# One-hots of every fourth column of an edge sort: from VectorE to ScalarE

## The chip, the cores and the metric

The kernel runs on one core of a Trainium2 chip. Five engines work there, each through its own queue of instructions in a fixed order, and they wait for each other by semaphores: PE (TensorE, matrix products into the PSUM banks), DVE (VectorE), ACT (ScalarE), POOL (GpSimd, here mostly gathers by indirect DMA) and SP (SyncE, which issues the other DMAs). The metric is the device time of one execution in microseconds, median of several.

## The reference, cut to what matters

Two graph layers run on 6,250 nodes with 256 features. The first is graph attention over 100,000 edges with 8 heads, the second attention over 131,072 other edges with 4 heads of 4 channels, whose result gates four experts' feed-forward networks. Both sum over the edges that end in a node:

```python
alpha = jax.nn.leaky_relu(a_src[src] + a_dst[dst], NEG_SLOPE)
ex = jnp.exp(alpha - amax[dst])
denom = jax.ops.segment_sum(ex, dst, num_segments=N)
attn = ex / (denom[dst] + 1e-16)
msg = h[src] * attn[:, :, None]
out = jax.ops.segment_sum(msg, dst, num_segments=N)
```

The first graph's edges come sorted by `dst`, the second's don't. The kernel sorts them itself, so that each chunk of 128 edges belongs to one tile of nodes. The sort doesn't depend on the first layer's result.

## The kernel before, in words

**Graph 1's loop.** The first layer runs over 104 groups of 8 chunks, one group a pass (`for i in range(NG1 + 1)` in every engine's program). POOL gathers the source rows of the 8 chunks (L722). DVE makes the scores of the pass (L1495 to L1517), ACT takes their exp (L870), and DVE multiplies the gathered rows by it in one instruction (L1523, `messages`). Then PE makes for each chunk one product that sums the messages by node (L1268), and DVE adds it to the accumulator (L1489, `add`). An add stands two chunks behind its product, so the last two adds of a pass come after the next scores. ACT also copies the transposes that PE makes of the next pass's selection matrices (L875). Of the 2,345 lines, `a` is ACT's queue, `v` DVE's and `pe` PE's.

**Graph 2's sort rides along.** `sort_order` lists the sort's steps with a cost for each, and a planner spreads them over 792 slots, one slot for each chunk of graph 1's first 99 passes (`sort_slots`). Every engine runs through the same slots, and takes from each step what is its own. In the last part of the sort there are 1,024 columns of 128 edges; a step there costs 400, and a slot gets two of them, now and then three.

**A column** j is placed by two matmuls (`place`, L1150 with 512 and L1151 with 64 columns) that multiply a one-hot of each edge's lane (`Av`) by a one-hot of its chunk's number (`Bv`), scaled by `bE`, which packs the edge's fields. `Av` comes four columns at a time: PE makes the codes into a bank ("hot", L1142), from a transpose that it makes for 16 columns ("turn", L1135, cast by ACT in L789), and ACT turns the bank into `Av` by a relu (L795). `Bv` is one instruction of DVE for each column (L2134, `onehots`): is the number 0 to 575 equal to `winF`, times `bE`.

**What sets the order.** `onehots` j stands two steps ahead of `place` j. There are four buffers `Bv`, so it waits (`p_pl`) until `place` j - 4 has read the same one. `place` j waits for its `Bv` (`v_bv`) and for its `Av` (`a_av`). Hot g stands in step 4g + 2, and needs the bank that ACT's relu of hot g - 1 has read. In each queue the sort's steps of a slot stand right behind the chunk's own work, and the exp and the copy of a pass stand ahead of its eight slots on ACT.

Of the kernel before, what the change touches and what calls it, by code (L numbers as in the profile page):

```python
# [13 lines left out]
HW = 576  # L14
# [22 lines left out]
def build(nc, x_d, src_d, dst_d, W_d, as_d, ad_d, bias_d, lns_d, lnb_d, Wg_d, gas_d, gad_d, bg_d, gam_d, bet_d,  # L37
          W1_d, b1_d, W2_d, b2_d, ei_d, out_d):
    f32, i32, u32, i16, u16, f16, b16 = (mybir.dt.float32, mybir.dt.int32, mybir.dt.uint32, mybir.dt.int16, mybir.dt.uint16,
                                          mybir.dt.float16, mybir.dt.bfloat16)  # L40
    ALU = mybir.AluOpType
    ACT = mybir.ActivationFunctionType
# [3 lines left out]
    with ctx:  # L46
        def sb(name, shape, dt=f32):
            return ctx.enter_context(nc.sbuf_tensor(name, shape, dt))
# [4 lines left out]
        def sem(name):  # L53
            return ctx.enter_context(nc.semaphore(name))

        def sems(names):
            return [sem(n) for n in names.split()]
# [39 lines left out]
        x_f = sb("x_sb", [128, T * D])  # L97
# [25 lines left out]
        ones = sb("ones", [128, 128])  # L123
# [3 lines left out]
        iota16 = sb("iota16", [128, NC2], f16)  # L127
# [71 lines left out]
        NB = 4  # L199
# [17 lines left out]
        laneI, winF, bE, u2 = x_f[:, 7808:8832].bitcast(i32), x_f[:, 8832:9856], x_f[:, 9856:10880], x_f[:, 10880:11904]  # L217
# [3 lines left out]
        nI, fI, fJ, fX, fY = xtmp(4, i32), xtmp(1, i32), xtmp(2, i32), xtmp(4, f32), xtmp(5, f32)  # L221
        Av = [x_f[:, 256 * n:256 * n + 256].bitcast(f16) for n in range(4)]
        Bv = [x_f[:, 1024 + 288 * n:1312 + 288 * n].bitcast(b16) for n in range(NB)]
        dcd = [x_f[:, 2176 + HW * n:2176 + HW * n + HW] for n in range(6)]

        def turn_at(k):

            return 5 * k + 2

        def hot_at(g):  # L230

            return 5 * (g // 4) + g % 4 + 3

        def hot_bank(g):

            return pbank[7 if g < HB // 4 + 2 else 5]
# [44 lines left out]
                e.wait_ge(v_out, outs(n))  # L281


        l_e1, l_e2, l_w, l_row, l_blk, p_tm, s_map1, s_map2, p_hot = sems("l_e1 l_e2 l_w l_row l_blk p_tm s_map1 s_map2 p_hot")
        l_h = sems("l_h0 l_h1 l_h2 l_h3")
        s_c, s_v, s_stage, s_cnt, p_tot, s_pair, s_flag, s_fold = sems(
            "s_c s_v s_stage s_cnt p_tot s_pair s_flag s_fold")
# [15 lines left out]
        s_lane, v_bv, a_av, p_pl, s_idx2 = sems("s_lane v_bv a_av p_pl s_idx2")  # L303
# [481 lines left out]
        def a_sort(a, op):  # L785
            if op[0] == "turn":
                k = op[1]
                a.wait_ge(p_hot, turn_at(k))
                a.copy(CT[k % 2], hot_bank(4 * k)[:, 0:128]).then_inc(a_av, 1)  # L789
            if op[0] == "hot":  # L790
                g = op[1]
                a.wait_ge(p_hot, hot_at(g))
                if g >= 4:
                    a.wait_ge(p_pl, 4 * (g - 3))
                a.activation(Av[g % 4], hot_bank(g)[:, :], ACT.Relu).then_inc(a_av, 1)  # L795

        def a_ffn(a, op):
            if op[0] == "up" and op[3] == 1:
# [300 lines left out]
        def p_sort(pe, op):  # L1099
            if op[0] == "cmask":  # L1100
                b = op[1]
                pe.wait_ge(v_mk, b + 1)
                for h in range(2):
                    t = pe.matmul(pbank[5 + h][:, :], Z16[:, 48 - b:176 - b], msk[b % 3][:, HB * h:HB * h + HB], start=b == 0, stop=b == T - 1)
                t.then_inc(p_mk, 1)
            if op == ("offsets", 0):
                pe.wait_ge(s_dg, 1)
                pe.matmul(pbank[7][:, 0:2 * T], ones[:, :], dg.rearrange("p w b -> p (w b)"), start=True, stop=True).then_inc(p_tot2, 1)
            if op[0] == "map":
                p_map_row(pe, g2, s_tm2, 1, (5, 6, 7))  # L1110
            if op[0] == "pmask":
                b = op[1]
                pe.wait_ge(v_mk, T + b + 1)
                if b == 0:
                    pe.wait_ge(s_base, 1)
                    pe.wait_ge(s_map2, 6)
                for h in range(2):
                    n = 2 * b + h
                    if n >= 3:
                        pe.wait_ge(v_pk, n - 2)  # L1120
                    pe.matmul(pbank[5 + n % 3][:, :], tri16, msk[(T + b) % 3][:, HB * h:HB * h + HB], start=True, stop=False)
                    pe.matmul(pbank[5 + n % 3][:, :], selq[:, b:b + 1].broadcast_to([128, 128]), base16[:, HB * h:HB * h + HB],
                              start=False, stop=True).then_inc(p_ps, 1)
            if op == ("codes", 8):
                pe.wait_ge(s_lane, 1)
                pe.matmul(pbank[7][:, 0:128], laneT.rearrange("p j b -> p (j b)"), ident16[:, :], start=True, stop=True).then_inc(p_hot, 1)
            if op[0] == "turn":
                k = op[1]
                if k == 0:
                    pe.wait_ge(s_lane, 2)  # L1130
                else:
                    pe.wait_ge(a_av, turn_at(k) - 2)
                if k == HB // 16 + 1:
                    pe.wait_ge(s_lane, 3)
                pe.matmul(hot_bank(4 * k)[:, 0:128], C16[k // 32][:, k % 32 * 128:k % 32 * 128 + 128], ident16[:, :],  # L1135
                          start=True, stop=True).then_inc(p_hot, 1)
            if op[0] == "hot":
                g = op[1]
                pe.wait_ge(a_av, hot_at(g) - 2)
                if g == HB // 4 + 2:  # L1140
                    pe.wait_ge(s_lane, 3)
                pe.matmul(hot_bank(g)[:, :], CT[g // 4 % 2], lanes[:, g % 4 * 512:g % 4 * 512 + 512], start=True, stop=True).then_inc(  # L1142
                    p_hot, 1)
            if op[0] == "place":
                j = op[1]
                n, w = j % NB, j // HB
                A = Av[j // 4 % 4][:, j % 4 * 128:j % 4 * 128 + 128]
                pe.wait_ge(v_bv, j + 1)
                pe.wait_ge(a_av, hot_at(j // 4 + (1 if j == HB else 0)) - 1)
                pe.matmul(pbank[5 + 2 * w][:, :], A, Bv[n][:, 0:512], start=j % HB == 0, stop=j % HB == HB - 1)  # L1150
                pe.matmul(pbank[6][:, 64 * w:64 * w + 64], A, Bv[n][:, 512:HW], start=j % HB == 0,  # L1151
                          stop=j % HB == HB - 1).then_inc(p_pl, 1)
# [797 lines left out]
        def v_sort(v, c, op, tile_counts):  # L1950
# [174 lines left out]
            if op == ("fields", 6):  # L2125
# [1 line left out]
                v.memset(g2.dl[:, :], 512.0).then_inc(*c.one())  # L2127
                v.memset(g2.dl16[:, :], 512.0).then_inc(*c.one())
                v.wait_ge(*c.now())
            if op[0] == "onehots":  # L2130
                j = op[1]
                if j >= NB:
                    v.wait_ge(p_pl, j - NB + 1)
                v.tensor_scalar(Bv[j % NB], iota16[:, 0:HW], winF[:, j:j + 1], bE[:, j:j + 1], ALU.is_equal, ALU.mult).then_inc(v_bv, 1)  # L2134
# [211 lines left out]
```

## Time and profile before

| | |
|---|---|
| time, median of 3 runs | 3172.53 us (3170.5 to 3176.74) |
| the profiled execution | 3174.1 us, span 3172.3 us |
| busy, share of the span | PE 74%, DVE 70%, POOL 59%, ACT 29% |
| graph 1's multiplies (L1523) | 104, from 159.9 to 1761.0 us |
| one-hots of chunk numbers (L2134) | 1,024 from 639.6 to 1662.3 us, 404.2 us in all |
| matmuls that use them (L1150) | 1,024, 396.9 us in all |

The trace gives for each instruction its start, its duration and what ended the idle time before it. "x2" is two instructions in one row, whose time is from the start of the first to the end of the last. Groups give the number of instructions, their busy time and the mean of one, and the idle time of the engine just before them. "Windows" are the busy times of each engine in a stretch, with the clock granted to PE, 1.00 being its full 2.4 GHz.

### The profile page before, as it was taken

The page shows a single profiled execution, that of the slowest core. Times are in us where ns is not written, and L with a number is a line of the kernel's source. Part 1 is how long each engine was busy: PE and PEld are TensorE (multiplying, and loading weights), DVE is VectorE, ACT ScalarE, POOL GpSimd, SP SyncE. Part 2 cuts the span into 40 slices and gives each one's busy share as a digit, 9 for nine tenths or more (in the row PEclk, how much of TensorE's full clock was granted, in tenths as well). Part 3 has the DMA queues.
Part 4 walks back from the last instruction along what each step waited for, and adds up shares of the span by engine and source line. Part 5 has one row for each costly group of instructions (what it writes and reads, how often), then busy time and mean ns, then how long its engine had stood idle before and what let it go on. Part 6 is the DMA issues. An engine that isn't in the chain of part 4 may idle for free. (4 is left out here: it accounts for less than half of the span.)

```text
span 3172.3 us, 41404 instructions
## 1 busy us (share of the span) xinstructions
PE 2356.1 (74%) x11166; PEld 1458.1 (46%) x11166; DVE 2228.5 (70%) x5853; ACT 904.8 (29%) x2255; POOL 1882.1 (59%) x1969
## 2 busy tenths in 40 slices
PE   2777776588888878888886675987788777887745
PEld 1444444344444444444444354544455444454434
DVE  7688887877777777777776775365566555656558
ACT  6510000022222212222220453333334332333313
POOL 0557666555555555555556225677777777777740
PEclk9888875688888878888886776998899988989877
DMA  4423333233333333333335101222323322222257
GB/s 148 131 82 104 92 99 85 72 86 86 86 84 86 86 84 86 84 86 86 83 84 154 34 4 23 78 66 59 75 60 73 73 58 60 64 62 67 63 166 273
DMA packets 168323, 271.99 MB, mean 86 GB/s; under 512 B 45430, under 2 KB 87988, under 8 KB 168084
## 3 DMA queue, kind: packets, MB, share of 16 engines
q0 software_dynamic: 67008, 127.12, 17.6%
q1 hardware_dynamic: 101076, 142.09, 13.8%
q8 instruction: 100, 1.64, 0.2%
q14 instruction: 139, 1.14, 0.1%
HBM read 228.24 MB, written 40.84 MB: 85 GB/s over the span
## 5 line engine op out<-in xcount | busy, mean ns | idle before, releaser
L722 POOL DMA_INDIRECT Gb<-table,idx x832 | 977.0, 1174 | 664.6 <-PE pb L1268 424.2
L1268 PE MATMUL pb<-Gb,Sall 128*128 128x264 f32 x1664 | 679.3, 521 | 238.4 <-DVE Gb L1523 182.5
L1268 PEld LDWEIGHTS pb<-Gb,Sall 128*128 128x128 f32 x1664 | 366.0, 248 | 378.5 <-DVE Gb L1523 203.2
L1489 DVE TENSOR_TENSOR big<-big,pb 128x264 f32 x832 | 352.6, 424 | 222.3 <-PE pb L1268 115.8
L1165 PE MATMUL pb<-big,early 128*128 128x512 f32 (+1 forms) x832 | 446.5, 643 | 50.8 <-ACT Gb L805 39.8
L1179 PE MATMUL pb<-early,Gb 128*128 128x256 f32 x1568 | 442.1, 430 | 48.0 <-ACT Gb L805 46.3
L2134 DVE TENSOR_SCALAR x_sb<-iota,x_sb 128x576 bf16<-128x576 f16 x1024 | 404.2, 428 | 93.8 <-PE pb L1151 89.2
L1150 PE MATMUL pb<-x_sb 128*128 128x512 bf16 x1024 | 396.9, 438 | 0.3 <-DVE x_sb L2134 0.3
L1179 PEld LDWEIGHTS pb<-early,Gb 128*128 128x128 f32 x1568 | 318.5, 214 | 128.4 <-ACT Gb L805 49.9
L656 POOL DMA_INDIRECT dl<-table,idx x288 | 282.5, 981 | 105.9 <-issue 93.9
L656 POOL DMA_INDIRECT tab<-table,idx x272 | 267.7, 984 | 85.2 <-issue 81.7
L656 POOL DMA_INDIRECT early<-table,idx x272 | 267.0, 982 | 82.9 <-issue 82.9
L795 ACT ACTIVATE x_sb<-pb 128x512 f16<-128x512 f32 x256 | 152.9, 597 | 538.1 <-PE pb L1142 535.4
L2201 DVE TENSOR_TENSOR idx<-pb,b2B 128x256 f32<-128x256 f32 x196 | 83.2, 424 | 301.5 <-PE pb L1179 301.1
L1523 DVE TENSOR_TENSOR Gb<-Gb 128x2048 f32<-128x2048 f32 x104 | 237.5, 2284 | 0.3 <-ACT Gb L870 0.3
L2273 DVE TENSOR_TENSOR acc<-acc,asall 128x20 f32 x832 | 149.9, 180 | 117.5 <-issue 21.3
L1252 PE MATMUL pb<-early,STb 128*128 x832 | 119.3, 197 | 145.9 <-DVE zc L1511 55.7
L805 ACT ACTIVATE Gb<-pb,b1c 128x512 f32<-128x512 f32 (+1 forms) x208 | 137.0, 662 | 315.1 <-PE pb L1165 314.4
L1151 PE MATMUL pb<-x_sb 128*128 128x64 bf16 x1024 | 212.7, 208 | 0.0
L870 ACT ACTIVATE Gb<-zb 128x64 f32<-128x64 f32 x104 | 26.7, 256 | 555.8 <-DVE zb L1517 555.8
L1165 PEld LDWEIGHTS pb<-big,early 128*128 128x128 f32 x832 | 134.5, 202 | 104.3 <-ACT Gb L805 48.2
L1252 PEld LDWEIGHTS pb<-early,STb 128*128 128x128 bf16 x832 | 80.1, 97 | 213.8 <-issue 185.5
(412 smaller groups left out, 3368.6 us busy)
## 6 DMA issues: line engine op xcount, KB each, us to landing
Sall<-dlT SPq DMA_DIRECT2D x208, 256.0 KB, 3.5
Y<-idx SPq DMA_DIRECT2D x96, 256.0 KB, 2.1
big<-Y SPq DMA_DIRECT2D x16, 1024.0 KB, 10.9
Gb<-table,idx POOLq DMA_INDIRECT x832
x_sb<-in_x_dram SPq DMA_DIRECT2D x8, 1536.0 KB, 13.7
out_dram<-x_sb SPq DMA_DIRECT2D x24, 256.0 KB
dl<-table,idx POOLq DMA_INDIRECT x288
tab<-table,idx POOLq DMA_INDIRECT x272
```

The lines of the kernel that those rows point to most:

```text
L656: g.indirect_dma_start(out=Gt2[s][:, k, :], out_offset=None, in_=g2.table, in_offset=bass.IndirectOffsetOnAxis(ap=g2.idx[:, c:c + 1], axis ...
L722: g.indirect_dma_start(out=G1[:, i % 2, k, :], out_offset=None, in_=g1.table, in_offset=bass.IndirectOffsetOnAxis(ap=g1.idx[:, c:c + 1], a ...
L795: a.activation(Av[g % 4], hot_bank(g)[:, :], ACT.Relu).then_inc(a_av, 1)
L1150: pe.matmul(pbank[5 + 2 * w][:, :], A, Bv[n][:, 0:512], start=j % HB == 0, stop=j % HB == HB - 1)
L1151: pe.matmul(pbank[6][:, 64 * w:64 * w + 64], A, Bv[n][:, 512:HW], start=j % HB == 0, stop=j % HB == HB - 1).then_inc(p_pl, 1)
L1165: t = pe.matmul(pbank[b][:, 0:nt * 128], W1s[:, w, k, f * 128:f * 128 + 128], xT[:, t0:t0 + nt, k * 128:k * 128 + 128], start=k == 0, stop ...
L1179: t = pe.matmul(pbank[b][:, 0:D], hh[:, bi % 2, f, j * 128:j * 128 + 128], W2s[:, w, f, :], start=f == 0, stop=f == 3)
L1252: t = pe.matmul(pbank[1][:, k * 48:k * 48 + 48], ST1[:, i % 2, k, :], tab31s[:, bass.ds(pe.snap(regs[k], min_val=0, max_val=T * 16), 16), ...
L1268: pe.matmul(sbank[c % 3][:, 0:g1.R], S1[:, (i - 1) % 2, k, :], G1[:, (i - 1) % 2, k, :], start=True, stop=True).then_inc(p_sum, 1)
L1489: v.tensor_tensor(o, o, sbank[n % 3][:, 0:g1.R], ALU.add).then_inc(v_add, 1)
L1523: v.tensor_tensor(hv, hv, G1[:, s, :, 256:264].unsqueeze(3).broadcast_to([128, CG, 8, 32]), ALU.mult).then_inc(v_msg, 1)
L2134: v.tensor_scalar(Bv[j % NB], iota16[:, 0:HW], winF[:, j:j + 1], bE[:, j:j + 1], ALU.is_equal, ALU.mult).then_inc(v_bv, 1)
```

## The change

For every column j with j % 4 = 3 ACT makes the one-hot, by three operations on 576 elements a partition: |winF - n|, then relu(1 - that), which is 1 where the numbers agree and 0 elsewhere, then times `bE`. Two temporaries, `winA` and `winB`, are shared by all columns. Each operation waits for the one before by a new semaphore `a_bv`, and the third for the same buffer as before, `Bv[3]`. DVE leaves these columns out, and PE waits for `a_bv` there.

```diff
+        winA, winB = x_f[:, 10880:11456], x_f[:, 11456:11744].bitcast(f16)
...
                 a.activation(Av[g % 4], hot_bank(g)[:, :], ACT.Relu).then_inc(a_av, 1)
+            if op[0] == "onehots" and op[1] % 4 == 3:
+
+                j = op[1]
+                if j == 3:
+                    a.wait_ge(s_lane, 2)
+                a.activation(winA, iota16[:, 0:HW], ACT.Abs, scale=-1.0, bias=winF[:, j:j + 1]).then_inc(a_bv, 1)
+                a.wait_ge(a_bv, 3 * (j // 4) + 1)
+                a.activation(winB, winA, ACT.Relu, scale=-1.0, bias=ones[:, 0:1]).then_inc(a_bv, 1)
+                a.wait_ge(a_bv, 3 * (j // 4) + 2)
+                if j >= NB:
+                    a.wait_ge(p_pl, j - NB + 1)
+                a.activation(Bv[3], winB, ACT.Copy, scale=bE[:, j:j + 1]).then_inc(a_bv, 1)
...
-                pe.wait_ge(v_bv, j + 1)
+                if j % 4 == 3:
+                    pe.wait_ge(a_bv, 3 * (j // 4) + 3)
+                else:
+                    pe.wait_ge(v_bv, 3 * (j // 4) + j % 4 + 1)
...
-            if op[0] == "onehots":
+            if op[0] == "onehots" and op[1] % 4 < 3:
```

**ACT's queue**, the whole of the pass whose multiply starts at 924.80 us in the trace (exp, copy, hot, turn, three hots, and the exp of the next), before:

```order
L870 ACTIVATE Gb<-zb 128x8x8 [waits v_z]
L875 CAST Sall<-pb 128x1024 [waits p_sum,p_tp]
L795 ACTIVATE x_sb<-pb 128x512 [waits p_pl,p_hot]
L789 CAST x_sb<-pb 128x128 [waits p_hot]
L795 ACTIVATE x_sb<-pb 128x512 [waits p_pl,p_hot] x3
L870 ACTIVATE Gb<-zb 128x8x8 [waits v_z]
```

The same pass after the change, up to its third hot (a hot is L796 now, the turn's cast L790, the exp L883):

```order
L883 ACTIVATE Gb<-zb 128x8x8 [waits v_z]
L888 CAST Sall<-pb 128x1024 [waits p_sum,p_tp]
L796 ACTIVATE x_sb<-pb 128x512 [waits p_pl,p_hot]
L790 CAST x_sb<-pb 128x128 [waits p_hot]
L802 ACTIVATE x_sb<-iota,x_sb 128x576
L804 ACTIVATE x_sb<-x_sb,ones 128x576 [waits a_bv]
L808 ACTIVATE x_sb<-x_sb 128x576 [waits p_pl,a_bv]
L796 ACTIVATE x_sb<-pb 128x512 [waits p_pl,p_hot]
L802 ACTIVATE x_sb<-iota,x_sb 128x576
L804 ACTIVATE x_sb<-x_sb,ones 128x576 [waits a_bv]
L808 ACTIVATE x_sb<-x_sb 128x576 [waits p_pl,a_bv]
L796 ACTIVATE x_sb<-pb 128x512 [waits p_pl,p_hot]
```

Between the turn and the next exp stand four triples and three hots in turn; the fourth triple is the last thing ahead of the exp. Other passes have three or four triples, and the places of turn and hots shift from pass to pass.

**DVE's queue**, from the multiply of that pass on, before (L1482 loads registers, L1488 and L1489 are an add):

```order
L1523 TENSOR_TENSOR Gb<-Gb 128x8x256 [waits a_ex]
L2134 TENSOR_SCALAR x_sb<-iota,x_sb 128x576 [waits p_pl] x4
L1482 TENSOR_LOAD tmr
L1488 ISA [waits v_add,p_sum]
L1489 TENSOR_TENSOR big<-big,pb 128x264
L2134 TENSOR_SCALAR x_sb<-iota,x_sb 128x576 [waits p_pl] x2
L1488 ISA [waits v_add,p_sum]
L1489 TENSOR_TENSOR big<-big,pb 128x264
L2134 TENSOR_SCALAR x_sb<-iota,x_sb 128x576 [waits p_pl] x2
```

And after:

```order
L1539 TENSOR_TENSOR Gb<-Gb 128x8x256 [waits a_ex]
L2150 TENSOR_SCALAR x_sb<-iota,x_sb 128x576 [waits p_pl] x3
L1498 TENSOR_LOAD tmr
L1504 ISA [waits v_add,p_sum]
L1505 TENSOR_TENSOR big<-big,pb 128x264
L2150 TENSOR_SCALAR x_sb<-iota,x_sb 128x576 [waits p_pl] x2
L1504 ISA [waits v_add,p_sum]
L1505 TENSOR_TENSOR big<-big,pb 128x264
L2150 TENSOR_SCALAR x_sb<-iota,x_sb 128x576 [waits p_pl]
```

Every other slot has one one-hot in place of two; nothing else on DVE moved.

**PE's queue**, the first slot of that pass, before:

```order
L1268 MATMUL pb<-Gb,Sall 128x264 [waits v_add,a_w32,v_msg]
L1150 MATMUL pb<-x_sb 128x512 [waits a_av,v_bv]
L1151 MATMUL pb<-x_sb 128x64
L1142 MATMUL pb<-x_sb 128x512 [waits a_av]
L1150 MATMUL pb<-x_sb 128x512 [waits a_av,v_bv]
```

And after:

```order
L1284 MATMUL pb<-Gb,Sall 128x264 [waits v_add,a_w32,v_msg]
L1166 MATMUL pb<-x_sb 128x512 [waits a_av,v_bv]
L1167 MATMUL pb<-x_sb 128x64
L1155 MATMUL pb<-x_sb 128x512 [waits a_av]
L1166 MATMUL pb<-x_sb 128x512 [waits a_av,a_bv]
```

PE's order is the same; every fourth placing matmul waits for ACT in place of DVE, and it is the next one behind a hot.

## Rows read from the trace of the kernel before

**Rows 1.** Windows, 640 to 1,670 us: busy us of PE, PEld, DVE, ACT, POOL
```profile
640.00:1670.00 1030.00, 838.16 (x4417) 491.72 (x4418) 809.45 (x1945) 250.21 (x446) 601.79 (x515) 0.82 0.32 85
```

**Rows 2.** Timeline of DVE in one pass: start, us, operation, idle before
```profile
924.80 2.28 DVE L1523 TENSOR_TENSOR Gb<-Gb 128x2048 f32<-128x2048 f32 x1
...
931.87 0.43 DVE L1489 TENSOR_TENSOR big<-big,pb 128x264 f32 x1 [1.63 <-issue]
...
932.89 0.42 DVE L1489 TENSOR_TENSOR big<-big,pb 128x264 f32 x1
...
937.47 0.76 DVE L2134 TENSOR_SCALAR x_sb<-iota,x_sb 128x576 bf16<-128x576 f16 x2
938.15 0.54 DVE L1495 TENSOR_REDUCE adt<-pb 128x128 f32<-128x384 f32 x1
...
940.33 0.43 DVE L1489 TENSOR_TENSOR big<-big,pb 128x264 f32 x1 [0.21 <-DVE big L1489]
940.68 2.28 DVE L1523 TENSOR_TENSOR Gb<-Gb 128x2048 f32<-128x2048 f32 x1
```

**Rows 3.** Timeline of PE in the same pass: sums of slots 0, 2, 4 and 6
```profile
927.14 1.25 PE L1268 MATMUL pb<-Gb,Sall 128*128 128x264 f32 x2 [2.01 <-DVE Gb L1523]
...
931.66 0.69 PE L1268 MATMUL pb<-Gb,Sall 128*128 128x264 f32 x2
...
933.91 0.69 PE L1268 MATMUL pb<-Gb,Sall 128*128 128x264 f32 x2
...
936.16 0.69 PE L1268 MATMUL pb<-Gb,Sall 128*128 128x264 f32 x2
```

**Rows 4.** Timeline of ACT in the same pass: first hot, turn, next exp
```profile
929.33 0.60 ACT L795 ACTIVATE x_sb<-pb 128x512 f16<-128x512 f32 x1 [3.16 <-PE pb L1142]
931.43 0.27 ACT L789 CAST x_sb<-pb 128x128 f16<-128x128 f32 x1 [1.51 <-PE pb L1135]
...
939.77 0.26 ACT L870 ACTIVATE Gb<-zb 128x64 f32<-128x64 f32 x1 [1.82 <-DVE zb L1517]
```

**Rows 5.** Groups of DVE, 640 to 1,670 us: count | busy, mean ns | idle before
```profile
L2134 DVE TENSOR_SCALAR x_sb<-iota,x_sb 128x576 bf16<-128x576 f16 x1024 | 404.2, 428 | 93.8 <-PE pb L1151 89.2
...
L1513 DVE SCALAR_TENSOR_TENSOR zc<-zc 128x64 f32<-128x64 f32 x64 | 14.4, 225 | 2.2
```

**Rows 6.** Groups of ACT by shape, whole span
```profile
L849 ACT ACTIVATE big<-big,small 128x782 f32<-128x782 f32 x38 | 35.4, 932 | 0.0
...
L951 ACT ACTIVATE idx<-ident,Sall 128x128 f32<-128x128 f32 x64 | 20.3, 392 | 3.7 <-DVE Sall L1708 3.7
L897 ACT ACTIVATE early<-big 128x256 f32<-128x256 f32 x49 | 19.6, 400 | 0.0
```

**Rows 7.** Timeline of ACT near the start: two operations without a wait between
```profile
15.51 0.93 ACT L849 ACTIVATE big<-big,small 128x782 f32<-128x782 f32 x1
16.34 0.19 ACT L849 ACTIVATION_READ_ACCUMULATOR big<-big,small 128x1 f32 x1
```

**Rows 8.** Timeline, eight passes: first multiply with its turn, and the last turn
```profile
829.61 2.28 DVE L1523 TENSOR_TENSOR Gb<-Gb 128x2048 f32<-128x2048 f32 x1
...
837.09 0.27 ACT L789 CAST x_sb<-pb 128x128 f16<-128x128 f32 x1 [0.52 <-PE pb L1135]
...
947.32 0.27 ACT L789 CAST x_sb<-pb 128x128 f16<-128x128 f32 x1 [1.51 <-PE pb L1135]
```

**Rows 9.** Timeline, eight passes: multiply and first hot, of the first and the last
```profile
701.66 2.28 DVE L1523 TENSOR_TENSOR Gb<-Gb 128x2048 f32<-128x2048 f32 x1
...
708.67 0.60 ACT L795 ACTIVATE x_sb<-pb 128x512 f16<-128x512 f32 x1 [5.46 <-PE pb L1142]
...
813.52 2.28 DVE L1523 TENSOR_TENSOR Gb<-Gb 128x2048 f32<-128x2048 f32 x1
...
818.05 0.60 ACT L795 ACTIVATE x_sb<-pb 128x512 f16<-128x512 f32 x1 [3.23 <-PE pb L1142]
```

**Rows 10.** Windows of PE, graph 2's stage: length, busy us, granted clock
```profile
2059.00:2060.00 1.00, 0.00 (x0) 1.00 0.11 16
```

More of the change, by code:

```diff
@@ L281, in wait_read @@
                 e.wait_ge(v_out, outs(n))
-        l_e1, l_e2, l_w, l_row, l_blk, p_tm, s_map1, s_map2, p_hot = sems("l_e1 l_e2 l_w l_row l_blk p_tm s_map1 s_map2 p_hot")
+        l_e1, l_e2, l_w, l_row, l_blk, p_tm, s_map1, s_map2, p_hot, a_bv = sems("l_e1 l_e2 l_w l_row l_blk p_tm s_map1 s_map2 p_hot a_bv")
         l_h = sems("l_h0 l_h1 l_h2 l_h3")
```

## The prediction, made before the changed kernel had run

> **What bounds the kernel now.** I first looked for the stretch that holds the edited work. The page's groups put the 1,024 one-hots (L2134) and the 1,024 matmuls that use them (L1150) between 640 and 1,670 us, and in that stretch DVE is busy for 809 of 1,030 us and PE for 838, but ACT for 250 only [rows 1]. Read as averages, ACT has room and DVE is short. An average does not say who is late, so next comes one pass of the loop over graph 1's chunks, in order of time.
>
> A pass is from one big multiply (L1523) to the next. I take the pass from M = 924.80 to 940.68, 15.88 us [rows 2]. DVE multiplies for 2.28 us, makes four one-hots, loads its registers (the 1.63 us before 931.87), and then works at a steady pace, one slot (one add, two one-hots) in 1.02 us (931.87, 932.89). At 938.15 it starts the scores of the next pass and 2.53 us later it multiplies again. PE [rows 3] starts its sums 2.34 us after M at the lower clock, so its first two slots take 4.52 us (927.14 to 931.66); later ones, at the full clock, take 2.25 us a pair (933.91, 936.16), in which PE doesn't pause. So from slot 2 on PE needs 2.25 us for two slots and DVE 2.04: they are nearly level, PE a little behind. That decides what relief of DVE is worth.
>
> ACT [rows 4] has in the same pass the exp (0.26), the copy of the transposes, the first conversion of a one-hot bank ("hot", L795, 0.60) at 929.33, a small cast ("turn", L789, 0.27) at 931.43, then three hots. It waits for PE before each. The exp of the next pass starts at 939.77 and the multiply that needs it at 940.68, so the exp could come 0.61 us later at no cost.
>
> **What the change removes, adds and moves.**
>
> DVE loses 256 of 1,024 one-hots of 0.428 us [rows 5], 110 us in all, about four a pass.
>
> ACT gains 256 times three operations on 128x576. No row shows such an operation. The nearest are 128x782 with a bias column at 932 ns and 128x128 with a scale column at 392 ns [rows 6]: (932 - 392) / 654 = 0.826 ns an element, so 392 + 448 x 0.826 = 762 ns. Without the column it would be some 90 ns less, from 128x256 at 400 ns: 400 + 320 x 0.826 = 664 ns. Each of the three here has a column, so I take 0.76, with 0.67 as the lower end. The second and the third wait for the one before. What ACT loses at such a wait is not in the trace; DVE loses 2.2 us before 64 chained operations, 0.034 us each [rows 5], and 0.21 us where its add waits for the last add (940.33) [rows 2]. I take 0.04, the row of the same kind of wait, and keep 0.21. An operation that doesn't wait starts 0.10 us before the end of the one ahead (15.51 + 0.93 to 16.34) [rows 7], which I take as 0.09 for the first of the three and for the hot behind them. So a column A costs 3 x 0.76 + 2 x 0.04 - 0.09 = 2.27 us and a hot 0.60 - 0.09 = 0.51.
>
> In sum ACT goes from 250 to about 250 + 256 x 2.28 = 834 us of the 1,030: no engine would be over its time. But A and hot are both in ACT's one queue, and PE waits for both: four columns cost ACT 2.27 + 0.51 = 2.78 us, and PE needs 2.25 us for the same four. At the full clock ACT sets the pace. It can't use PE's pause to get ahead, since there is one buffer for its one-hot (the third operation waits until the matmul four columns before has read it), and hot waits for a matmul of PE that comes after the pause.
>
> What is queued behind A decides the price: the exp of the next pass. I follow ACT through the pass of M = 924.80, by its new order: exp, copy, hot, turn, A, hot, A, hot, A, hot, A, exp. Hot and turn wait for PE as before, so the turn ends at 931.43 + 0.27 = 931.70, M + 6.90. Then come four A and three hots, 9.08 + 1.53 = 10.61, end at M + 17.51, and exp and hand-over (0.26 + 0.04) put the next multiply at M + 17.81, where it is now at M + 15.88: 1.93 us later. DVE's own way (last one-hot released by PE, then 2.53) comes earlier than that, so its saving is not seen in such a pass.
>
> The place of hot and turn drifts from pass to pass, so I did the same for eight passes in a row from M = 829.61 [rows 8]. Turns are 7.48, 8.92, 7.21, 8.08, 6.95, 6.35, 6.63 and 6.64 us after M; behind the turn are three A and three hots (8.34 us) in the first five, four A and three hots (10.61) in the next two, four and four (11.12) in the last. Turn + 0.27 + that + 0.30 gives 16.39, 17.83, 16.12, 16.99, 15.86, 17.53, 17.81 and 18.33, against passes of 14.80, 16.81, 15.30, 16.43, 16.07, 15.78, 15.88 and 17.04 now. Counting a shorter one as no change, the sum is 8.96 us, 1.12 a pass.
>
> Other passes have the turn later, with more hots ahead of it. For the eight from M = 701.66 [rows 9] I start at the first hot, 7.01, 6.42, 6.24, 6.53, 5.01, 5.01, 4.53 and 4.53 us after M. Behind it are three A, three hots and the turn with some 0.43 us of waiting (9.04 us) in the first five, one A more in the sixth, 11.31 in the seventh and 11.82 in the eighth. With 0.60 and 0.30 that gives 16.95, 16.36, 16.18, 16.47, 14.95, 17.22, 16.74 and 17.25, against 16.12, 16.70, 15.24, 16.25, 15.33, 15.87, 16.35 and 16.09: 4.89 us, 0.61 a pass.
>
> The mean of the two is 0.87 us. Some 62 passes hold columns: 62 x 0.87 = +54 us. With 0.67 us an operation each A is 0.27 shorter, 3.3 of them lie on the path, and a pass loses about 0.2 us, +12 in all; with 0.21 us a wait each is 0.34 longer, 1.1 a pass, and it is +122.
>
> At nothing I cost the copy of the transposes (it follows the exp as before, and PE waits for the longer multiply anyhow), the gathers of POOL (busy for 602 of 1,030 us [rows 1]) and the wait of the matmuls on ACT instead of DVE, which is priced as the pace. Passes outside 640 to 1,670 us and the later stages are untouched.
>
> The first row against the change is DVE's own: one instruction of 0.428 us does the compare and the multiply, and three of ACT of 0.76 us replace it, 5.3 times the time [rows 5, 6]. The Trainium skill, "ScalarE: Activation LUTs", section "Rules for kernel authors", sends relu, max and multiply to VectorE, which it calls up to about 3x faster per element in bf16. By that ratio, taken whole for each of the three, an A would be an estimated 3 x 3 x 0.428 = 3.9 us, and 62 x 3.3 x 1.6 = 330 us more would be lost; the rows show 1.8 times for one operation, so that is left aside.
>
> **The rivals.**
>
> *ACT keeps up, and DVE's relief counts.* If the three operations overlap more than I think, or the exp is late by less than its 0.61 us, the pass ends where PE and DVE let it. The last pair of one-hots on DVE starts as soon as the add before it is done (937.47); with one of two gone, scores begin at most 0.35 to 0.42 us earlier, since the other still waits for PE's slot before. That is 62 x 0.35 = 22 us, 3,151. More isn't there, because PE's 2.25 us a pair stay; for it speaks that ACT is idle for 76% of the stretch, and that in three of sixteen passes my chain ends early by itself. It decides if four columns cost ACT under about 2.3 us.
>
> *Nothing that can be measured.* Passes that win and lose cancel, 3,172: it needs A at about 1.9 us.
>
> *PE drops to the lower clock in mid-pass.* The new waits (0.5 us a pair) could add to its pause. A pair at the lower level takes 4.52 us in place of 2.78; three such pairs a pass are +5.2, 62 x 5.2 = +320, 3,550 or so. Against it: through a pause of over 1 us between dense matmuls (all of 2,059 to 2,060) the granted clock stayed at 1.00 [rows 10].
>
> **How the numbers follow.** The profiled execution took 3,174.1 us (span 3,172.3), 1.6 over the median 3,172.53. 3,174.1 + 54 - 1.6 = 3,226. ACT sets the pace and delays the exp: 0.66. ACT keeps up and DVE's relief counts: 0.22. Nothing: 0.07. Lower clock: 0.05. The likeliest case alone reaches from 3,185 (+12) to 3,296 (+122). Both signs hold chances, so the range goes down into the second case, to 3,155, and up to 3,300; left out are half of the gain, the clock and an edge. A difference of 0.2% (6 us) is about what can be told from none. Faster 0.22; same 0.10, the third case and the low edge of the first; slower 0.68.
>
> **What would show it.** In the changed profile, ACT's three lines at 0.76 us each, with little idle time before them; the waits of the matmul that uses a one-hot should be on ACT, about 0.5 us a pair; the exp should be late, so that the multiply L1523 (now at another line) waits for ACT; passes of 16.7 us instead of 15.9, and unchanged in the other stages. DVE should be idle more, not done sooner. I am wrong if the three operations take under 2.0 us together, if the multiply doesn't wait for the exp, or if PE's first slots, at the lower clock, move.

## The result, and the profile after it

The changed kernel takes 3241.06 us (median of 4 runs, 3240.27 to 3246.3), the kernel before on the same chip 3174.64 (3170.5 to 3177.93): ratio 1.021, 95% interval 1.0193 to 1.0227, so **66 us slower**. A second comparison gave 3247.9 against 3174.59, ratio 1.0227 (1.0211 to 1.0242). The forecast was 3226.

The first thing to read is where the 66 us are. Each pass of the loop has one multiply of graph 1 (now L1539). From the 32nd multiply to the 97th, which spans all columns, 65 passes took 1665.16 - 625.24 = 1039.9 us before and 1732.98 - 624.90 = 1108.1 now, 68.2 more. The 30 passes ahead of them took 452.5 and 453.5, the six behind 84.2 and 84.4. What lies ahead of the first multiply and behind the last moved by 3 us or less. The 65 passes are called the stretch below.

Windows of the changed kernel over the stretch (length, busy us of PE, PEld, DVE, ACT, POOL, granted clock), to be read beside [rows 1]:

```profile
640.00:1735.00 1095.00, 819.89 (x4332) 466.99 (x4408) 732.31 (x1687) 789.68 (x1213) 591.38 (x515) 0.87 0.30 80
```

DVE is relieved as meant, ACT is three times as busy as before, and none of the engines is busy for the whole of the window.

A second trace of the kernel before (before_again below) recorded nearly as many matmuls in its window, so PE's busy times can be compared:

```profile
640.00:1670.00 1030.00, 828.89 (x4339) 492.94 (x4419) 809.21 (x1946) 250.11 (x446) 602.33 (x515) 0.82 0.32 85
```

The window of the changed kernel is 65 us longer. PE is idle in it for 74 us more (275 against 201) and busy for 9 us less, at a mean granted clock of 0.87 against 0.82. So the loss is waiting, and a little of it came back through the clock.

Groups of the page of the changed kernel (count | busy, mean ns | idle before, with what ended it), beside [rows 5]:

```profile
L2150 DVE TENSOR_SCALAR x_sb<-iota,x_sb 128x576 bf16<-128x576 f16 x768 | 314.7, 433 | 224.8 <-PE pb L1167 221.4
L1166 PE MATMUL pb<-x_sb 128*128 128x512 bf16 x945 | 355.4, 423 | 103.6 <-ACT x_sb L808 103.2
...
L1539 DVE TENSOR_TENSOR Gb<-Gb 128x2048 f32<-128x2048 f32 x104 | 237.9, 2287 | 13.3 <-ACT Gb L883 13.3
...
L808 ACT ACTIVATE x_sb<-x_sb 128x576 bf16<-128x576 f16 x256 | 198.3, 775 | 14.0 <-PE pb L1167 5.9
L804 ACT ACTIVATE x_sb<-x_sb,ones 128x576 f16<-128x576 f32 x256 | 198.5, 775 | 8.4
```

Here the change is seen whole. PE now waits 103 us for ACT's one-hots, 0.66 us for each of 157 waits, where it waited 0.3 us in all for any one-hot before. DVE's one-hots, fewer by a quarter, wait for the matmuls that release their buffers for 221 us instead of 89 [rows 5]. DVE's 90 us of saved work came back as 132 us of waiting. But the multiply waits for the exp for 13 us only.

One pass in order of time, that of [rows 2 to 4], which starts now at 942.62. First ACT (start, us, operation, idle before), then PE, then DVE:

```profile
949.03 0.78 ACT L802 ACTIVATE x_sb<-iota,x_sb 128x576 f32<-128x576 f16 x1
949.84 0.77 ACT L804 ACTIVATE x_sb<-x_sb,ones 128x576 f16<-128x576 f32 x1
950.65 0.78 ACT L808 ACTIVATE x_sb<-x_sb 128x576 bf16<-128x576 f16 x1
951.33 0.58 ACT L796 ACTIVATE x_sb<-pb 128x512 f16<-128x512 f32 x1
...
954.09 0.58 ACT L796 ACTIVATE x_sb<-pb 128x512 f16<-128x512 f32 x1
...
956.86 0.58 ACT L796 ACTIVATE x_sb<-pb 128x512 f16<-128x512 f32 x1
...
959.62 0.24 ACT L883 ACTIVATE Gb<-zb 128x64 f32<-128x64 f32 x1
```

```profile
951.48 0.39 PE L1166 MATMUL pb<-x_sb 128*128 128x512 bf16 x1 [1.41 <-ACT x_sb L808]
```

```profile
942.62 2.29 DVE L1539 TENSOR_TENSOR Gb<-Gb 128x2048 f32<-128x2048 f32 x1 [0.53 <-ACT Gb L883]
...
952.71 0.77 DVE L2150 TENSOR_SCALAR x_sb<-iota,x_sb 128x576 bf16<-128x576 f16 x2 [1.80 <-PE pb L1167]
...
956.95 0.54 DVE L1511 TENSOR_REDUCE adt<-pb 128x128 f32<-128x384 f32 x1
...
959.89 2.29 DVE L1539 TENSOR_TENSOR Gb<-Gb 128x2048 f32<-128x2048 f32 x1 [0.32 <-ACT Gb L883]
```

ACT works without a pause in steps of 2.76 us (951.33, 954.09, 956.86) for four columns, for which PE took 2.25 [rows 3]. PE stands 1.41 us until L808 is done, and DVE 1.80 us until PE has read its buffer. DVE reaches its scores 14.33 us after the multiply instead of 13.35 [rows 2]. So in this pass everything behind the turn runs at ACT's pace, DVE's own path too, and the exp adds 0.32 us.

The other group of passes shows a second route. Start of a pass at M = 739.70, whose last matmul of the old pass waits for ACT, whose lookups are late, and whose copy of the transposes is late in turn:

```profile
738.23 0.19 PE L1167 MATMUL pb<-x_sb 128*128 128x64 bf16 x1 [0.56 <-ACT x_sb L808]
740.20 1.23 PE L1268 MATMUL pb<-early,STb 128*128 x8 [1.78 <-issue]
741.26 1.03 PE L1274 MATMUL pb<-ident,STb 128*128 128x128 bf16 x8
```

```profile
742.33 1.01 ACT L888 CAST Sall<-pb 128x1024 f32<-128x1024 bf16 x1 [3.28 <-PE pb L1274]
743.24 0.78 ACT L802 ACTIVATE x_sb<-iota,x_sb 128x576 f32<-128x576 f16 x1
```

The copy stands ahead of ACT's next triple in the queue. It ends at M + 3.6, where it ended at M + 1.4 in the same pass before (over all passes 1.2 to 2.7, middle 1.5, before, and 1.2 to 4.7, middle 2.6, now). So the triple starts late. Over the stretch ACT waits 129.7 us for the transposes (83.4 before).

### The profile page after: what moved, and what is told of

The parts are those of the page before. It is cut to its first block and busy times, and to the rows that moved or that the text cites. A ratio compares the mean times of both kernels' runs of the same rounds, so it can differ in the third digit from the quotient of the medians.

```text
span 3238.5 us, 42092 instructions
## 1 busy us (share of the span) xinstructions
PE 2344.5 (72%) x11087; PEld 1437.1 (44%) x11166; DVE 2151.2 (66%) x5597; ACT 1445.1 (45%) x3023; POOL 1868.0 (58%) x1969
## 5 line engine op out<-in xcount | busy, mean ns | idle before, releaser
L723 POOL DMA_INDIRECT Gb<-table,idx x832 | 967.2, 1163 | 744.1 <-PE pb L1284 521.8
L1284 PE MATMUL pb<-Gb,Sall 128*128 128x264 f32 x1664 | 659.7, 508 | 177.9 <-DVE Gb L1539 121.9
L1284 PEld LDWEIGHTS pb<-Gb,Sall 128*128 128x128 f32 x1664 | 358.7, 242 | 313.4 <-DVE Gb L1539 141.1
L2150 DVE TENSOR_SCALAR x_sb<-iota,x_sb 128x576 bf16<-128x576 f16 x768 | 314.7, 433 | 224.8 <-PE pb L1167 221.4
L1166 PE MATMUL pb<-x_sb 128*128 128x512 bf16 x945 | 355.4, 423 | 103.6 <-ACT x_sb L808 103.2
L657 POOL DMA_INDIRECT tab<-table,idx x272 | 264.6, 973 | 84.2 <-issue 82.3
L883 ACT ACTIVATE Gb<-zb 128x64 f32<-128x64 f32 x104 | 26.2, 252 | 495.3 <-DVE zb L1533 495.3
L1539 DVE TENSOR_TENSOR Gb<-Gb 128x2048 f32<-128x2048 f32 x104 | 237.9, 2287 | 13.3 <-ACT Gb L883 13.3
L1166 PEld LDWEIGHTS pb<-x_sb 128*128 128x128 f16 x1024 | 108.9, 106 | 256.8 <-ACT x_sb L808 182.1
L808 ACT ACTIVATE x_sb<-x_sb 128x576 bf16<-128x576 f16 x256 | 198.3, 775 | 14.0 <-PE pb L1167 5.9
L804 ACT ACTIVATE x_sb<-x_sb,ones 128x576 f16<-128x576 f32 x256 | 198.5, 775 | 8.4
```

Source lines behind the costliest of these rows:

```text
L657: g.indirect_dma_start(out=Gt2[s][:, k, :], out_offset=None, in_=g2.table, in_offset=bass.IndirectOffsetOnAxis(ap=g2.idx[:, c:c + 1], axis ...
L723: g.indirect_dma_start(out=G1[:, i % 2, k, :], out_offset=None, in_=g1.table, in_offset=bass.IndirectOffsetOnAxis(ap=g1.idx[:, c:c + 1], a ...
L804: a.activation(winB, winA, ACT.Relu, scale=-1.0, bias=ones[:, 0:1]).then_inc(a_bv, 1)
L808: a.activation(Bv[3], winB, ACT.Copy, scale=bE[:, j:j + 1]).then_inc(a_bv, 1)
L1284: pe.matmul(sbank[c % 3][:, 0:g1.R], S1[:, (i - 1) % 2, k, :], G1[:, (i - 1) % 2, k, :], start=True, stop=True).then_inc(p_sum, 1)
L1539: v.tensor_tensor(hv, hv, G1[:, s, :, 256:264].unsqueeze(3).broadcast_to([128, CG, 8, 32]), ALU.mult).then_inc(v_msg, 1)
```

## The experiments

The runs were made in three sets: ops0 to ops4; exp_ahead, lead4, every8 and lead8; and the last four. In the first two sets, on two chips, every kernel, the one before too (medians 3683.87 and 3692.39), took 510 to 520 us longer. The third set, on one of those chips, was without it. I call this the slower condition. Most of it lies in graph 2's stage: from graph 1's last multiply to the end of the span ops0 took 1,895 us and the kernel before, in its own set, 1,411. The first 30 passes took 453 to 457 us there as well.

But the stretch isn't free of it. ACT's waits in ops0, which has no triple on ACT (640 to 1,672 us; "remote" is a wait whose end the trace puts down to no instruction):

```profile
ACT Sall L883 <- remote: 70.6, 23, 5.1
ACT x_sb L796 <- remote: 56.4, 13, 5.4
```

Over the stretch such waits are 127 us in ops0, 137 in ops1, 80 in ops2, 129 in lead4, 76 in every8, 132 in lead8, 9 in exp_ahead and none in ops4. None of the six traces outside the condition has a single one. The kernel before has no trace in the condition. From each of the eight traces its stretch there can be estimated, as the stretch less what that profiled execution took over before's median: 1,046 to 1,066 us, 6 to 26 more than the 1,040 outside it. So I compare times within a set, and a stretch of the first two sets with one outside them to no better than some 20 us. Within a condition, two traces of the same changed kernel differ by 7.7 us in the stretch (1108.1 and 1115.8), two of before by 0.6. Each run is set against the runs of before around it, so a ratio can differ by 0.2% from that of the medians.

PE clock is the mean granted clock from 640 us to the end of the stretch.

| kernel | ratio to before (95%) | stretch, us | PE clock |
|---|---|---|---|
| ops0 | 0.9959 (0.9931 to 0.9987) | 1034.3 | 0.84 |
| ops1 | 1.0054 (1.0031 to 1.0076) | 1073.7 | 0.82 |
| ops2 | 1.0076 (1.0052 to 1.01) | 1091.9 | 0.81 |
| ops4 | 1.0703 (1.0668 to 1.0739) | 1306.8 | 0.84 |
| exp_ahead | 1.0084 (1.0051 to 1.0117) | 1094.4 | 0.88 |
| lead4 | 1.0132 (1.0098 to 1.0166) | 1121.5 | 0.80 |
| every8 | 1.0049 (1.0022 to 1.0077) | 1092.6 | 0.82 |
| lead8 | 1.0045 (1.0022 to 1.0068) | 1076.4 | 0.82 |
| after_again | 1.0227 (1.0211 to 1.0242) | 1115.8 | 0.86 |
| copy_late | 1.031 (1.0294 to 1.0326) | 1138.8 | 0.88 |
| best8 | 0.9902 (0.9884 to 0.9921) | 1006.9 | 0.87 |
| before_again | one run, 3173.99 us | 1039.3 | 0.82 |

### How many operations ACT can take: 0, 1, 2 and 4

**ops0** leaves ACT's triple out altogether, and PE's wait for it (it waits for the first, empty one-hot only). DVE's relief stays. ops0, ops1 and ops2 so leave the edges of every fourth column out of graph 2; behind the last multiply they took 1,888 to 1,895 us, and the complete kernels of the same condition 1,886 to 1,901, so the lack of these edges isn't seen in the time.

```diff
-                a.activation(winA, iota16[:, 0:HW], ACT.Abs, scale=-1.0, bias=winF[:, j:j + 1]).then_inc(a_bv, 1)
...
-                a.activation(Bv[3], winB, ACT.Copy, scale=bE[:, j:j + 1]).then_inc(a_bv, 1)
+                if j == 3:
+                    a.activation(Bv[3], iota16[:, 0:HW], ACT.Copy, scale=0.0).then_inc(a_bv, 1)
```

> Of the changed kernel, ACT's three operations for every fourth column are left out (its one-hot is zero throughout, so those edges are left out of graph 2; DVE's work is that of the changed kernel). It is DVE's relief without ACT's work. Theory P (ACT sets the pace of four columns, 2.76 us against PE's 2.25): 3,150 to 3,173, since nothing on ACT is left to wait for, and DVE's relief is worth 0 to 22 us. Rival R (DVE's time is what bounds a pass): 62 passes x 1.7 us less, near 3,070.

Measured: ratio 0.9959, 15 us less than before (by the medians, 3676.56 and 3683.87, it is 7). So 256 one-hots taken off DVE without any price are worth 0.4% (0.1 to 0.7%), though DVE's group of one-hots is some 90 us shorter without them (404.2 to 314.7 in the changed kernel). DVE's wait for PE shows where the rest went (waits of ops0, 640 to 1,690 us: us, times, longest):

```profile
DVE x_sb L2145 <- PE pb L1162: 142.2, 173, 2.2
```

It was 89.2 before [rows 5]. This gives the rival in which relief counts its size, 15 us in this condition. A bound by DVE's time, some 105 us (theory R), is refuted.

**ops1** keeps the third operation (and its wait for the buffer), **ops2** the second and third, **ops4** has one relu more. The edit of ops4, the other two take lines away in the same place:

```diff
                 a.activation(winA, iota16[:, 0:HW], ACT.Abs, scale=-1.0, bias=winF[:, j:j + 1]).then_inc(a_bv, 1)
-                a.wait_ge(a_bv, 3 * (j // 4) + 1)
+                a.wait_ge(a_bv, 4 * (j // 4) + 1)
+                a.activation(winC, winA, ACT.Relu, scale=-1.0, bias=ones[:, 0:1]).then_inc(a_bv, 1)
+                a.wait_ge(a_bv, 4 * (j // 4) + 2)
```

> The same with one operation of ACT for each fourth column, which waits for the buffer as the third one does (its input is zero, those edges are left out). P: four columns cost ACT 1.3 us, under PE's 2.25, so the same as with no operation, within 6 us. Rival L (each operation costs its share, by hand-over or by ACT's time as such): a third of the loss, 22 us over the kernel with none.

> The same with two chained operations of ACT for each fourth column (relu and multiply; the output is zero, those edges are left out). P: four columns cost ACT 2.08 us, just under 2.25, so within 10 us of the kernel with none. L: two thirds of the loss, 44 us over the kernel with none.

> The changed kernel, complete, with a fourth chained operation (a relu into a temporary that nobody reads). P: four columns cost ACT 3.57 us in place of 2.76, 0.81 more for some 3.3 to 4.1 groups a pass in 62 passes: 165 to 206 us over the changed kernel, 3,405 to 3,447. L: 22 us over it, 3,263.

Measured, over ops0: with one operation 22 us by the medians (0.95% by the ratios, 35 us), with two 38 (1.2%), and with four 268 (7.4%). The changed kernel, with three, lies 66 to 73 us over before in the other condition, and ops4 261 us over before in this one. So from three to four it is 187 to 194 us, and the stretch grows by 191 to 199. A fourth operation costs ACT 256 x 0.80 = 205 us, so nearly all of it lies on the path. PE and DVE wait accordingly (waits of ops4, 640 to 1,640 us, which is not yet its whole stretch):

```profile
PE pb L1169 <- ACT x_sb L811: 189.3, 137, 2.3
```

```profile
DVE x_sb L2153 <- PE pb L1170: 289.4, 203, 3.8
```

From three operations to four the pace theory is right, and an equal price for each operation is refuted. Below three, the pace theory misses: by it one and two operations (four columns at 1.3 and 2.1 us, under PE's 2.25) were to cost at most 6 and 10 us, and they cost 22 and 38. The equal price has 22 for the first right, by the medians. What the 22 us are isn't shown. PE waits for ACT's one-hot in ops1 for 8.5 us only. It is busy for 843.4 us in ops1's window and for 823.0 in ops0's, with as many matmuls recorded (4,440 and 4,431), at a mean granted clock of 0.82 against 0.84: 20 of the 39 us by which the stretch is longer are PE's busy time. The group of ops1's single operation and its copy (640 to 1,690 us) have waits for PE, and some of the condition's:

```profile
L807 ACT ACTIVATE x_sb<-x_sb 128x576 bf16<-128x576 f16 x249 | 192.6, 774 | 37.2 <-PE pb L1166 34.7 <-issue 1.8
...
L887 ACT CAST Sall<-pb 128x1024 f32<-128x1024 bf16 x64 | 64.8, 1012 | 211.2 <-PE pb L1283 80.8 <-remote 80.1 <-PE pb L1273 50.3
```

The operation stands behind a copy and hots that wait for PE, with one buffer that PE releases. That such places in the queue cost the 22 us is a guess that this run doesn't show. Whether they are paid outside the slower condition, in which ACT stands still for reasons that the trace doesn't name, wasn't run. The next runs change the places.

### Places in the queue: exp_ahead, lead4, every8, lead8

**exp_ahead** holds a triple that falls into the last slot of a pass back until the next exp is issued, so that the exp never stands behind it.

```diff
+                for op in held:
+                    a_sort(a, op)
+                held = []
...
-                        a_sort(a, op)
+                        if k == CG - 1 and op[0] == "onehots":
+                            held.append(op)
+                        else:
+                            a_sort(a, op)
```

> The changed kernel, but on ACT a triple that falls in the last slot of a pass stands behind the exp instead of ahead of it. Theory E (the loss is the exp that comes late, as the prediction priced it): up to 62 x 0.9 = 56 us less, 3,185 to 3,230. Theory P (PE waits for the one-hot, DVE for PE's release; the multiply waited for the exp for 13 us in all): 13 us less at most, 3,228 to 3,241.

Measured: 1.0084. DVE's multiply waits for ACT for 0.3 us, and yet PE waits for ACT's one-hots as before, 99 us (groups of exp_ahead's page):

```profile
L2157 DVE TENSOR_SCALAR x_sb<-iota,x_sb 128x576 bf16<-128x576 f16 x768 | 314.4, 433 | 223.9 <-PE pb L1174 211.3
...
L1546 DVE TENSOR_TENSOR Gb<-Gb 128x2048 f32<-128x2048 f32 x104 | 237.8, 2287 | 3.4 <-issue 3.1
```

In time it is 31 to 34 us over before, by the ratio and by the medians, and the changed kernel 66 to 73 in the other condition: 32 to 42 us less. That is far more than the 13 us of the wait. The stretch is 14 to 21 us shorter than in the two traces of the changed kernel, and the condition may hide up to some 20 more. By the mark set for after_again (its expectation stands below: 0.9% or more above this ratio if theory E holds; it is 1.4%) this speaks for E, the exp as the forecast priced it, and against the 13 us. But the changed kernel has no run in this condition, and no wait in the trace shows where the gain would come from; the mean granted clock is 0.88 here, 0.86 and 0.87 there. How much the late exp costs, 13 us or some 40, the runs leave open.

**lead4** gives ACT three buffers of its own and starts each triple eight steps earlier.

```diff
+        Ba = [Bv[3], x_f[:, 11904:12192].bitcast(b16), x_f[:, 12192:12480].bitcast(b16)]
...
+                if -2 <= j < 2 * HB + -2:
+                    ops.append(("early", j + 2))
...
-                if j >= NB:
-                    a.wait_ge(p_pl, j - NB + 1)
-                a.activation(Bv[3], winB, ACT.Copy, scale=bE[:, j:j + 1]).then_inc(a_bv, 1)
+                if j >= 12:
+                    a.wait_ge(p_pl, j - 12 + 1)
+                a.activation(Ba[j // 4 % 3], winB, ACT.Copy, scale=bE[:, j:j + 1]).then_inc(a_bv, 1)
```

> The changed kernel with three buffers for ACT's one-hots instead of one, and ACT's triple eight steps (four slots) earlier in its queue. P, by its reason (ACT can't use PE's pause to get ahead): the waits of the placing matmul for ACT (103 us) mostly go, 3,150 to 3,190. E, and any theory by which ACT's share of the queue as such is the loss: 3,225 to 3,245, as the same operations are still ahead of the exp.

Measured: 1.0132, and the loss has moved. Groups of lead4's page:

```profile
L1171 PE MATMUL pb<-x_sb 128*128 128x512 bf16 x1024 | 400.3, 440 | 0.4 <-DVE x_sb L2155 0.4
...
L1544 DVE TENSOR_TENSOR Gb<-Gb 128x2048 f32<-128x2048 f32 x104 | 238.1, 2290 | 69.1 <-issue 40.4
```

PE no longer waits for ACT's one-hots (103 us in the changed kernel), but the multiply now stands idle for 69 us, 28 of them put down to the exp and 40 to nothing that the profile names. Some of that is the condition's: in ops0, without any triple, the multiply is idle for 24 us, and in before for none. In time it is 49 us over before, where the changed kernel is 66 to 73. Theory P misses: it expected 3,150 to 3,190, and the ratio makes it 3,216. The multiply waits for the exp for 28 us here and for 13 in the changed kernel, so the exp behind a triple holds the loop more. And the matmuls took longer. Windows of exp_ahead and lead4, of the same set and with as many matmuls:

```profile
640.00:1731.00 1091.00, 827.57 (x4428) 466.89 (x4427) 736.82 (x1701) 792.74 (x1215) 602.54 (x520) 0.88 0.30 81
```

```profile
645.00:1764.00 1119.00, 866.18 (x4432) 503.95 (x4432) 744.24 (x1702) 791.25 (x1217) 577.61 (x520) 0.80 0.30 79
```

PE is idle for 11 us less in lead4 and busy for 39 us more, at 0.80 of its clock in place of 0.88. So against exp_ahead its 28 us are a slower PE and not a longer wait. Why the granted clock fell isn't shown.

**every8** gives ACT every eighth column in place of every fourth, and **lead8** that with two buffers and the eight steps of lead. The core of every8:

```diff
-            if op[0] == "onehots" and op[1] % 4 == 3:
+            if op[0] == "onehots" and op[1] % 8 == 7:
```

> ACT makes the one-hot of every eighth column only, DVE the others, with one buffer each as before. P: eight columns cost ACT 3.3 us against PE's 4.5, so it isn't the pace: 3,155 to 3,178. L: half of the loss, 3,207.

> Every eighth column on ACT, two buffers of its own, eight steps earlier in its queue. P: no wait for ACT at all, and DVE's relief of two one-hots a pass counts as far as it can: 3,150 to 3,173, at or under the kernel with every eighth column alone. L: 3,207.

Measured: 1.0049 and 1.0045, intervals that overlap nearly whole. Eight columns cost ACT 2.27 + 2 x 0.51 = 3.3 us and PE 4.5, so the pace is no longer ACT's, and most of the loss is gone. What stays is a half per cent, 17 to 21 us, as with ops1 and in the same condition. In every8 PE still waits for ACT's one-hots (waits, 640 to 1,640 us); in lead8 no matmul waits for one of them, and yet it is no faster, though its stretch is 16 us shorter.

```profile
PE pb L1166 <- ACT x_sb L808: 25.2, 47, 0.8
```

### The copy, the repeats and a combined version

**copy_late** is the changed kernel with the copy of the transposes behind the sort work of three slots instead of ahead of all.

```diff
-                if i < NG1:
-                    a.wait_ge(p_tp, i + 1)
...
+                    if k == 3 and i < NG1:
+                        a.wait_ge(p_tp, i + 1)
```

> The changed kernel with ACT's copy of the transposes behind the fourth slot's start (after the sort work of three slots) instead of right behind the exp. In the trace of the changed kernel that copy ends 1.7 to 3.6 us after the multiply starts, and the first triple of a pass stands behind it. Theory C (part of the loss is ACT's queue standing still at the copy, for PE's late transposes, and is paid again by the placing matmul that needs the triple): 15 to 40 us less than the changed kernel. Theory P alone (four columns at 2.76 us, all of it): within 6 us of it.

Measured: 1.031, 26 us slower than after_again beside it (3273.43 against 3247.9). A miss. The waits of ACT over 640 to 1,735 us tell why, first after_again, then copy_late:

```profile
ACT Sall L888 <- PE pb L1274: 133.2, 64, 3.8
ACT x_sb L796 <- PE pb L1155: 72.5, 51, 3.1
```

```profile
ACT x_sb L796 <- PE pb L1155: 187.6, 65, 5.3
...
ACT x_sb L808 <- PE pb L1167: 28.7, 11, 3.0
...
ACT Sall L889 <- PE pb L1274: 1.9, 1, 1.9
```

ACT's wait at the start of a pass only changed its name, from the transposes to the first hot, because PE is late with both. And the copy, 1.0 us, has moved from that pause to the part of the pass in which ACT sets the pace. The stretch grew by 23 to 31 us, 0.35 to 0.47 us a pass. I read it so that the late copy is a sign of PE's lateness; what is shown is that moving it alone doesn't help.

**after_again** and **before_again** are the two kernels once more, without an edit.

> The changed kernel once more, so that it has a ratio and a trace beside the other runs on the chip they share. 1.5 to 2.3% slower than before if its loss doesn't depend on the chip. If P holds and the reordered exp brings 13 us at most, this ratio stands 0 to 0.4% above that of the kernel with the exp ahead (1.0084); if E holds, 0.9% or more above it.

> The kernel before once more, for its trace on this chip: the stretch of the 62 passes with columns. P and L expect it level with the kernel without ACT's operations, within 10 us.

They gave 1.0227 and 3173.99 us.

**best8** combines the steps so far: every eighth column, two buffers with eight steps of lead, the copy behind three slots, and an early triple of the last slot behind the exp. It differs from lead8 by the last two:

```diff
+                    if k == 3 and i < NG1:
+                        a.wait_ge(p_tp, i + 1)
...
+                        if k == CG - 1 and op[0] == "early":
+                            held.append(op)
```

> Every eighth column on ACT with two buffers eight steps ahead, the copy late and the exp ahead of the last slot's triple, all together. If P, C and E name all that ACT's operations cost, nothing is left of it and this stands at the kernel without ACT's operations, 0.2 to 0.4% under before. If some cost comes with any operation on ACT (L, seen as 20 us with one operation), it stays at or above before.

Measured: 3141.71 us, ratio 0.9902 (0.9884 to 0.9921), **33 us faster than the kernel before** and 106 faster than the changed one. It leaves nothing out. Both theories missed: one had 0.2 to 0.4% under before, the other at or above it. Its gain, too, lies in the stretch (1006.9 against 1039.3). Groups of its page:

```profile
L2162 DVE TENSOR_SCALAR x_sb<-iota,x_sb 128x576 bf16<-128x576 f16 x896 | 360.0, 432 | 100.7 <-PE pb L1179 96.7
...
L1178 PE MATMUL pb<-x_sb 128*128 128x512 bf16 x945 | 352.1, 418 | 0.0
...
L1551 DVE TENSOR_TENSOR Gb<-Gb 128x2048 f32<-128x2048 f32 x104 | 237.8, 2287 | 0.3 <-ACT Gb L887 0.3
```

No matmul waits for a one-hot, no multiply for the exp, and DVE's waits for PE are back at 97 us. ACT's copy sits where it waits for nothing (timeline of ACT, M = 699.07):

```profile
705.55 0.60 ACT L799 ACTIVATE x_sb<-pb 128x512 f16<-128x512 f32 x1 [4.86 <-PE pb L1165]
706.05 1.01 ACT L896 CAST Sall<-pb 128x1024 f32<-128x1024 bf16 x1
706.94 0.79 ACT L805 ACTIVATE x_sb<-iota,x_sb 128x576 f32<-128x576 f16 x1
```

Where the 33 us come from is told by PE's row, to be read beside before_again's above:

```profile
640.00:1631.00 991.00, 794.47 (x4318) 471.56 (x4394) 766.58 (x1812) 513.90 (x827) 587.89 (x512) 0.87 0.33 87
```

The window is 39 us shorter. PE is busy for 34 us less with as many matmuls recorded, and idle for 5 us less (197 against 201), at a mean granted clock of 0.87 against 0.82. Matmuls that use a one-hot took 418 ns in the mean, 433 in before_again:

```profile
L1150 PE MATMUL pb<-x_sb 128*128 128x512 bf16 x945 | 365.0, 433 | 0.3 <-DVE x_sb L2134 0.3
```

So the gain is mostly a faster PE and not a shorter wait. What raised the granted clock, the order on ACT or DVE's relief, isn't shown. Nor do ops0 and lead8 decide it: they gained 0.4% and lost 0.45% in the slower condition, with over 120 us of ACT's unnamed waits. Neither lead8 outside it nor the kernel before with the two moves and no column on ACT was run.

## Why the prediction was right, point by point

**The direction and the likeliest case held.** 3226 was forecast, 3241 measured, in the range. ACT's pace is the cause: with no triple the loss is gone (ops0), and one more operation costs nearly its full time (ops4). The road from there to the multiply was in large part another.

**The price of an operation: right.** 0.76 us forecast from a fit through [rows 6], 769, 775 and 775 ns measured; the gap at a self-wait 0.03 (949.03 + 0.78 to 949.84), 0.04 forecast; a step of triple and hot 2.76, forecast 2.78. The Trainium skill, "ScalarE: Activation LUTs", section "Rules for kernel authors", has VectorE up to about 3x faster per element in bf16. Here one operation took 775 ns against 433 of DVE on as many elements, 1.8 times, inside that bound.

**The pass followed in time: nearly right.** M + 17.81 forecast for the pass of 924.80, M + 17.27 measured. The eight passes from 829.61 took 137.02 us instead of 128.11, 8.91 more, where 8.96 was forecast. That closeness is partly luck, since the step below is wrong.

**"DVE's own way comes earlier than that, so its saving is not seen": failed.** The price was taken at one place only, the exp behind the last triple. In that very pass DVE's way was late by itself: scores at M + 14.33 in place of 13.35, so 0.98 of the 1.39 us came by PE's wait for L808 and DVE's wait for PE's release, and the exp added 0.32. Over the kernel the multiply waited for the exp for 13 us of the 68; I had priced the whole loss there, and had named a multiply that doesn't wait for the exp as a sign of being wrong. exp_ahead leaves open that the exp's place costs more than this wait (up to some 40 us).

**The mis-sized term: 0.61 us a pass for the other eight.** There the exp alone gave 4.89 us for eight passes. They took 704.17 to 841.27, 137.10 us, for 127.95 before: 9.15, or 1.14 a pass. With it 62 x 0.87 = 54 becomes 62 x 1.13 = 70, and the stretch measured 68. A triple that ends late delays the matmul, this the lookups and transposes, these the copy and the next triple: that is how the rows of M = 739.70 read, and copy_late shows that the copy can be taken out of this chain without a gain.

**"At nothing I cost the copy of the transposes": failed.** It waited 130 us instead of 83. copy_late showed that it isn't the cause either.

**The rivals.** *DVE's relief counts*: 15 us in ops0, where 22 was my price for it. *Nothing measurable*: it needed 1.9 us for four columns' one-hot; ops1 and ops2, cheaper than that, and every8 all cost 0.5 to 0.8% against before, in the slower condition. *PE's clock drops in mid-pass*: it did not. The granted clock of the stretch is 0.87, higher than before's 0.82 [rows 1]. I had it as a risk only; that it could rise and give time back, or decide between two variants (lead4, best8), I hadn't seen.

**The threshold.** I let the price begin where four columns cost ACT more than some 2.3 us. ops1, ops2 and every8, all below, lose 0.5 to 0.8% against before. The steep part does begin there (the changed kernel +2.1%, ops4 +7%). Below it lies a price that I hadn't, which best8, outside the slower condition, doesn't show.

## What to carry to other kernels

When work moves to an idle engine, compare periods, not shares: what its queue needs for one period of the loop, waits for the engine that feeds it included, against the slowest engine's period. In a loop whose engines hand buffers round, a late producer is paid for everywhere (PE's wait, then DVE's, then the copy), so price the ring and not only the instruction behind it. First run the version in which the moved work costs nothing: here it showed that 0.4% was there to win. The one version that won gave the helper half as much, its own buffers, and a place behind what others wait for; which of these won isn't shown. And split PE's row into busy and idle before you explain a gain: in lead4 and best8 the granted clock moved more than the waits did.

## What the runs showed of the hardware

- Three chained ACT operations of 128x576 with a bias or scale column took 769, 775 and 775 ns in the mean in the changed kernel, with f16 to f32, f32 to f16 and f16 to bf16. One that waits for its forerunner starts 0.03 to 0.04 us after its end, one that doesn't starts 0.10 to 0.11 us before it (L796 at 951.33).
- PE's pauses of 1.41 and 0.56 us in the middle of the pass of M = 942.62 didn't lower the granted clock: it read 1.00 from 951 to 960 us. Over the stretch the changed kernel had 74 us more of idle PE than before and a higher mean, 0.87 against 0.82.
- The same matmuls took 433 ns in the mean at 0.82 (before_again) and 418 at 0.87 (best8). PE's busy time in the windows of the two was 828.9 and 794.5 us.
- In two of three sets, on two chips, all kernels ran 510 to 520 us longer, most of it in graph 2's stage, with the first 30 passes of graph 1 unchanged within 1%. In seven of the eight traces taken then ACT stood idle in the stretch for 9 to 137 us, up to 5.8 us at a time, with no instruction named as the cause; in the six others never. Why is not known.
